# Eleven in place of ten one-hot tables for the first two blocks of a recommendation tower, with the third block's layers, the row numbers and the last loads moved

## The reference

```python
e = jnp.stack([tbl_0[ids[:, 0]], ..., tbl_25[ids[:, 25]]], axis=1)      # (2048, 26, 128)
all_emb = jnp.concatenate([bottom_output[:, None, :], e], axis=1)       # 27 features
gram = jnp.einsum('bfd,bgd->bfg', all_emb, all_emb)
z = gram[:, _TRIU_I, _TRIU_J]                                           # 351 products
h = jnp.concatenate([z, r_bottom_output], axis=1)                       # 479
h = jnp.maximum(h @ W_top1 + b_top1, 0.0)                               # 512
h = jnp.maximum(h @ W_top2 + b_top2, 0.0)                               # 256
y = h @ W_top3                                                          # 1
```

## Time and profile before

| | |
|---|---|
| profiled execution, its own time | 374.2 us |
| span, first to last instruction | 372.4 us |
| TensorE matmul busy | 339.9 us (91%) |
| TensorE weight load busy | 274.7 us (74%) |
| VectorE busy | 237.7 us (64%) |
| ScalarE busy | 231.8 us (62%) |
| GpSimd busy | 255.2 us (69%), gathers 252.1 |
| mean granted TensorE clock | 0.977 |
| chain that ended last | GpSimd 35%, TensorE 29%, issue 16%, VectorE 14% |

### The profile page before, as it was taken

How to read it: one execution, slowest core, us unless ns; L and a number is a source line. 1 busy time by engine, 2 the same in 40 slices (tenths; PEclk the granted TensorE clock), 3 DMA queues, 4 the chain that set the end, 5 groups by cost and what they waited for, 6 DMA issues and landing times.

```text
span 372.4 us, 8273 instructions
## 1 busy us (share of the span) xinstructions
PE 339.9 (91%) x3348; PEld 274.7 (74%) x3348; DVE 237.7 (64%) x276; ACT 231.8 (62%) x297; POOL 255.2 (69%) x258
## 2 busy tenths in 40 slices
PE   0899999998799999999799998999999983979997
PEld 0688777776578788888687886786888682867776
DVE  2999999999658769988599962423352223221542
ACT  3599988787887849689978744355533562131322
POOL 5778777777777777777777877777777777740020
PEclk9999999999789999999899999999999998899999
DMA  7867787664848898788765637742696354221110
GB/s 209 231 200 213 200 242 230 196 186 138 276 133 257 340 316 220 227 243 238 235 154 166 211 107 226 296 116 67 168 323 216 74 135 130 52 79 44 39 43 2
DMA packets 48391, 66.86 MB, mean 180 GB/s; under 512 B 15874, under 2 KB 34820, under 8 KB 47842
## 3 DMA queue, kind: packets, MB, share of 16 engines
q1 hardware_dynamic: 40126, 49.46, 44.3%
q0 software_dynamic: 8064, 16.35, 15.9%
q10 hardware_dynamic: 164, 0.52, 0.4%
HBM read 52.37 MB, written 13.93 MB: 178 GB/s over the span
## 4 chain that ended last, share of the span: by engine, by line
POOL 35%; PE 29%; issue 16%; DVE 14%; ACT 3%; DMA 2%; SPq 0%; ACTq 0%; DVEq 0%
POOL rows L559 35%; DVE onehot L827 11%; PE acc L587 8%; PE acc L588 7%; PE gram L618 4%; PE acc L623 3%; PE acc L625 2%; PE acc L624 2%; PE turned L600 2%; DVE table_lo L819 2%; DMA row_number<-in_row_numbers 2%; PE acc L662 1%; DVE pairs_lo L819 1%; ACT h L717 1%; DMA rows<-in_tbl,index 1%
## 5 line engine op out<-in xcount | busy, mean ns | idle before, releaser
L559 POOL DMA_INDIRECT rows<-in_tbl,index x248 | 252.1, 1017 | 78.0 <-issue 75.0
L827 DVE TENSOR_SCALAR onehot<-wanted,row_number 125x1029 fp32r<-125x1029 int32 x126 | 153.2, 1278 | 9.5 <-PE acc L588 9.4
L587 PE MATMUL acc<-onehot,table_hi 125*128 125x512 f32 x336 | 137.0, 408 | 12.4 <-DVE onehot L827 10.8
L588 PE MATMUL acc<-onehot,table_lo 125*128 125x512 f32 x288 | 115.8, 402 | 0.0
L587 PEld LDWEIGHTS acc<-onehot,table_hi 125*128 125x128 f32 x336 | 64.7, 193 | 28.5 <-issue 10.8
L618 PEld LDWEIGHTS gram<-features 128*54 128x54 f32 x2048 | 59.5, 134 | 15.3 <-issue 11.5
L618 PE MATMUL gram<-features 128*54 128x52 f32 x2048 | 65.5, 220 | 2.7 <-ACT features L696 1.7
L717 ACT ACTIVATE h<-wanted,row_number 125x1029 f32<-125x1029 int32 x42 | 48.8, 1163 | 26.2 <-PE acc L588 24.3
L588 PEld LDWEIGHTS acc<-onehot,table_lo 125*128 125x128 f32 x288 | 55.9, 194 | 12.5
L600 PE MATMUL turned<-identity,rows 128*128 128x128 f32 x248 | 40.7, 293 | 12.5 <-DMA rows<-in_tbl,index 6.8
L720 ACT ACTIVATE onehot<-h,row_number 125x1029 fp32r<-125x1029 f32 x42 | 48.6, 1157 | 1.4
(11 more groups left out here) (45 smaller groups left out, 279.5 us busy)
## 6 DMA issues: line engine op xcount, KB each, us to landing
wanted<-in_onehot_ids SPq DMA_DIRECT2D x21, 514.5 KB, 4.6
parked<-staged SPq DMA_DIRECT2D x32, 256.0 KB
table_raw<-in_tbl SPq DMA_DIRECT2D x17, 448.0 KB
looked<-parked SPq DMA_DIRECT2D x2, 2816.0 KB
square<-products SPq DMA_DIRECT2D x64, 84.5 KB
rows<-in_tbl,index POOLq DMA_INDIRECT x248
looked<-parked SPq DMA_DIRECT2D x1, 2560.0 KB
pairs<-in_tbl SPq DMA_DIRECT2D x3, 448.0 KB
```

Source lines behind the costliest of these rows:

```text
L559: pool.indirect_dma_start(out=rows[:, n % ROWS_RING, i, :], out_offset=None, in_=gathered[f], in_offset=bass.IndirectOffsetOnAxis(ap=index ...
L587: pe.matmul(to, table_hi[0:ROW_PARTS, v % HIGH_RING, c, :], of, start=(c == 0), stop=False)
L588: last = pe.matmul(to, raw_table(v, low=True)[0:ROW_PARTS, c, :], of, start=False, stop=(c == CHUNKS - 1))
L827: dve.tensor_scalar(onehot[0:ROW_PARTS, columns_of(v, c)], ids_of(v, slice(0, ROW_PARTS)), row_number[0:ROW_PARTS, c:c + 1], None, ALU.is_ ...
```

## The change

The number of looked-up tables becomes eleven for all blocks, so blocks 0 and 1 have 15 gathers per tile too (240 in all) and there are 22 visits, eleven of them ahead of the first gram chunk. `LAYERS_AT` for the last block becomes 8 and `ROUNDED_BEFORE` becomes a value per block, 6 for the last. `row_number` is loaded by GpSimd, as its first instruction, and no longer by SyncE. Part 3's pairs are loaded after the last chunk of tile 14, for three tiles, and part 4's after the last chunk of tile 15, for that tile only. Of the last tile's four stores two are issued by SyncE and two by ScalarE.

```diff
--- before.py
+++ after.py
@@ -19,7 +19,7 @@
 
 
 ONEHOT = [3, 4, 9, 13, 14, 17, 20, 21, 22, 23, 24]
-LOOKUPS = (10, 10, 11, 11)
+LOOKUPS = (11, 11, 11, 11)
 ALWAYS, MOST = min(LOOKUPS), max(LOOKUPS)
 ONEHOT_ROWS = 1000
 CHUNKS = 8
@@ -121,14 +121,14 @@
 
 
 
-LAYERS_AT = (None, 10, 10, 10)
+LAYERS_AT = (None, 10, 10, 8)
 
 
 
 LOOKUPS_AMONG = (16, 8, 8, 8)
 
 
-ROUNDED_BEFORE = 8
+ROUNDED_BEFORE = (None, 8, 8, 6)
 
 
 def products_and_others():
@@ -217,12 +217,14 @@
 
 
 
+
+LAST_LOT = (len(PARTS) - 1, BLOCK_TILES - 1, BLOCK_TILES)
 PAIRS_AFTER = {}
 for b in range(BLOCKS - 1):
     PAIRS_AFTER["gram", (b + 1) * BLOCK_TILES - 1, 1] = (b, 0, EARLY_TILES)
     PAIRS_AFTER["gram", (b + 1) * BLOCK_TILES - 1, TILE_CHUNKS - 1] = (b, EARLY_TILES, BLOCK_TILES)
-PAIRS_AFTER["gram", TILES - 1, 1] = (len(PARTS) - 2, 0, EARLY_TILES)
-PAIRS_AFTER["gram", TILES - 1, TILE_CHUNKS - 1] = (len(PARTS) - 1, EARLY_TILES, BLOCK_TILES)
+PAIRS_AFTER["gram", TILES - 2, TILE_CHUNKS - 1] = (len(PARTS) - 2, 0, BLOCK_TILES - 1)
+PAIRS_AFTER["gram", TILES - 1, TILE_CHUNKS - 1] = LAST_LOT
 
 
 
@@ -491,7 +493,7 @@
 
                 sp.wait_ge(act_products, chunks_taken(ACT_CHUNKS, (t + 1) * TILE_CHUNKS))
                 sp.wait_ge(dve_products, chunks_taken(DVE_CHUNKS, (t + 1) * TILE_CHUNKS))
-                for s in range(PACK):
+                for s in range(PACK if t < TILES - 1 else HELD):
                     store_place(sp, t, s)
 
             def load_pairs(part, first, end):
@@ -505,7 +507,6 @@
 
             load_index(0)
             load_wanted(0)
-            sp.dma_start(row_number[:], row_numbers).then_inc(row_number_landed, 16)
             load_raw(1)
             load_wanted(1)
             load_raw(2)
@@ -544,6 +545,7 @@
 
         @block.gpsimd
         def _(pool):
+            pool.dma_start(row_number[:], row_numbers).then_inc(row_number_landed, 16)
             pool.memset(identity[:], 0.0).then_inc(identity_zero, 1)
             pool.wait_ge(identity_zero, 1)
             pool.affine_select(out=identity[:], in_=identity[:], compare_op=ALU.not_equal, fill=1.0,
@@ -565,7 +567,7 @@
                 pool.wait_ge(square_landed[t % PRODUCTS_RING], (t // PRODUCTS_RING + 1) * PACK * 16)
             pool.wait_ge(accumulated, FILL["layer1", last_on_tiles_of(part), M1 - 1] + 1)
             for i in range(SP_LOADS, len(TRIPLES)):
-                load_triple(pool, *PARTS[part], i, last_pairs_landed)
+                load_triple(pool, PARTS[part][0], *LAST_LOT[1:], i, last_pairs_landed)
 
         @block.tensor
         def _(pe):
@@ -701,6 +703,13 @@
                 act.wait_ge(grammed, t * TILE_CHUNKS + j + 1)
                 at_least(act, square_landed[t % PRODUCTS_RING], (t // PRODUCTS_RING) * PACK * 16)
                 take_products(nc.scalar.copy, t, j).then_inc(act_products, 1)
+
+            def store_rest(t):
+
+                act.wait_ge(act_products, chunks_taken(ACT_CHUNKS, (t + 1) * TILE_CHUNKS))
+                act.wait_ge(dve_products, chunks_taken(DVE_CHUNKS, (t + 1) * TILE_CHUNKS))
+                for s in range(HELD, PACK):
+                    store_place(act, t, s)
 
             def table_high_part(v):
                 act.wait_ge(raw_landed[raw_place(v)], raw_count(v))
@@ -796,6 +805,8 @@
                 elif kind == "gram":
                     if y in ACT_CHUNKS:
                         products_out(x, y)
+                    if (x, y) == (TILES - 1, TILE_CHUNKS - 1):
+                        store_rest(x)
                     if (x, y) == (BLOCK_TILES, 0):
                         act.wait_ge(w1_landed, 16)
                         nc.scalar.copy(w1_hi[:], w1_raw[:]).then_inc(weights_high, 1)
@@ -889,7 +900,7 @@
                     fill_slot0(x)
                 elif kind == "gram":
                     b, q = divmod(x, BLOCK_TILES)
-                    if b and q * TILE_CHUNKS + y == ROUNDED_BEFORE:
+                    if b and q * TILE_CHUNKS + y == ROUNDED_BEFORE[b]:
                         split_pairs(b - 1)
                     if y in DVE_CHUNKS:
                         products_out(x, y)
```

## The result

| | before | after |
|---|---|---|
| median of the comparison | 374.44 us | 381.60 us |
| ratio, 95% interval | | 1.0195 [1.0121, 1.0269] |
| the same kernel run again, with others | 374.16 us | 379.98 us, 1.0154 [1.0121, 1.0188] |
| profiled execution, own time / span | 374.2 / 372.4 | 381.6 / 379.8 |
| mean granted TensorE clock | 0.977 | 0.972 |

The change makes the kernel slower by 1.5 to 2% (the two intervals span 1.2 to 2.7%). The forecast was 375.6 us with a range up to 379.5; the time lies above it.

A forecast was written before the change was run, and what follows sets the result against it. TensorE's own work was taken to set the pace up to about 307 us, then the gathers to 334. Span 372.4 + 8.3 - 0.7 - 0.6 - 1.9 - 9.9 + 1.1 + 1.0 + 3.1 + 1.0 = 373.8, plus 1.8: 375.6 us, range 369 to 379.5.

The forecast's parts named there:

- the pause ahead of t7.3: End of block 0's grams: transposes t7.3, moved ahead of chunk G4.0, wait for a ScalarE copy, +1.1 us.
- The extra visit: Before the first gram chunk: one more table visit, paced by VectorE, costs +8.3 us, ends 7.7 and 8.9.
- The waits that go: Last block: TensorE's pauses and the low clock behind them go, all but two copy waits, -9.9 us.
- the pairs wait: Third block's first layer piece: TensorE waits for tile 11's split pairs, +3.1 us, ends 2.6 and 3.6, or 0.
- +1.0 for the clock: Third block's layer piece: TensorE's clock is low behind the wait for split pairs, +1.0 us.
- 2.3 forecast: Behind tile 11's last chunk: 15 fewer transposes at 0.155 us each, -2.3 us.
- The row numbers: Kernel start: loaded by GpSimd they land sooner, so VectorE's first split comes earlier, -1.9 us, ends 0 and -1.9.
- case 4: Kernel start: row numbers come no sooner, GpSimd's descriptors waiting for VectorE or starting slowly; 377.5 us, chance 0.11.
- One copy fewer ahead of the first chunk: Between last lead visit and first gram chunk: six transpose groups, not seven, save one ScalarE copy, -0.6 us.
- case 3: Clock falls at all three new pauses (t7.3, t11.3, layer piece), 1.5 us each; 379.1 us, chance 0.13.
- The pause at tile 11: Tile 11: t11.3 waits 1.7 us for t11.1's copy while a shorter copy wait disappears, +1.0 us.

The follow-up runs named there:

- The kernel after again: The changed kernel, unchanged, measured a second time against the kernel before: 379.98 us, ratio 1.0154 [1.0121, 1.0188].
- The table of six: Changed kernel, third block's layers at chunk 10, 9, 8, against the kernel before: ten tables for blocks 0 and 1 1.0002, 0.9954, 0.9849; eleven 0.9991, 1.0033, 1.0154.

## Why the prediction was wrong

The step that failed is block 0. Between its first chunk and block 1's the sum has one term, +1.1 for the pause ahead of t7.3, and 5.1 us were measured. It has nothing there for the clock, which it let fall only behind the layer piece, and nothing for a load that lands late. The two small gains ahead of it, -1.9 and -0.6, did not come either. By the rows of the table the miss is 1.1 + 1.2 + 4.0 - 0.3 = 6.0 us.

1. **The extra visit, +8.3: right.** 8.3 in the lead; the splits stand (76.12 - 51.25)/3 = 8.3 apart as in the earlier trace rows.
2. **The waits that go, -9.9, and the pairs wait, +3.1 with +1.0 for the clock: right.** From tile 11's last chunk on the terms add up to -8.1, and -8.1 was measured. It holds for the parts as well: with eleven tables and the layers at chunk 10 this stretch takes 63.6 us, 12.0 less than before (9.9 + 2.3 forecast), and the early layers add 3.9 (4.1 forecast). The layer was reached 320.90 - 313.3 = 7.6 us behind tile 11's last chunk (7.7 forecast) and its piece was done 14.2 behind it (13.8 forecast). The last gather started at 324.0, not 320.1: the first came 0.8 later and the spacing was 1.33. It didn't matter.
3. **The row numbers, -1.9: failed.** The load's landing was taken from the loads of pairs at the end (2.3 to 2.7 us), when the nearest row was another load of the start, `wanted`, 5.8 us after its issue. It landed 6.1 after its issue. The first visit started 0.8 earlier, and that scatters as much from kernel to kernel. 1.1 us too much. It is the outcome of case 4 (no sooner), but nothing shows the mechanism of that case: SyncE's loads of the same table landed as late.
4. **One copy fewer ahead of the first chunk, -0.6: failed.** ScalarE still makes five copies of turns between its last one-hot build and the first placing copy, as before. With six transposes fewer TensorE only waits longer for the same copies: 3.31 ahead of the transposes where 2.67 stood, and 1.57 ahead of the chunk where 0.26 stood. 1.2 us in all.
5. **Block 0, +1.1 forecast and +5.1 measured: the largest part of the miss.** From start to start on TensorE, the 5.1 are these. From G3.3 to G4.0, where the pause at t7.3 stands, +2.1: the pauses at t7.2 and t7.3 are 2.01 + 1.20 against 1.91, and t7.3's transposes, now ahead of G4.0, took 0.88. The low clock at the first two chunks, +0.9, and in the visit behind them, +0.5 (8.14 against 7.64). At and in the fourth visit +1.8: a wait of 0.49 for the split of a table and one of 0.73 for ScalarE's copy of an accumulator. The rest is -0.2. The last two causes stay open. For the low clock see "The kernel after again". The table landed late, but that doesn't follow from the change: its cast comes 2.1 us behind the start of the two chunks ahead (146.81 - 144.66) and 0.3 before, yet 2.7 with ten tables and the layers at chunk 8 and 0.5 with ten tables and the layers at chunk 10, two kernels with the same steps up to there.
6. **The clock.** "After a pause of 1.91 the granted clock was 0.73" was held to be one place; I counted a fall only behind the layer piece. It fell behind t7.3 too, to 0.54 and for longer than before, but not behind tile 11's pauses of 0.41 and 1.20, where it was 1.00. Against the kernel before, the fall at t7.3 costs 1.3 us more (about 2.5 against 1.2; 1.0 of it shows in G4.0 and the visit behind it, 11.0 us against 10.0). So case 3 had the mechanism right at two of its three places and a fair price, 1.5, for one. That its 379.1 is the nearest to the measured time is mostly luck, since most of the miss lies elsewhere. The Trainium skill, TensorE: Matmul & The Clock Gate, section "HAM oscillation — how this bites in real kernels", tells of a kernel in which each wait for data between two groups of matmuls brings the low level back. Its waits are longer than the three new pauses here, of which two were followed by a fall and one was not.
7. **The pause at tile 11, +1.0: right in size.** The pauses are 0.41 and 1.20. From G7.3 to G8.0 it takes 3.2 us more, of which 1.7 are the eleven moved transposes; a copy wait of 0.67 behind it is gone; 0.8 are left. That the whole stretch to tile 11's last chunk grew by 2.4, near the 2.7 forecast, is partly luck: 1.0 of it is the low clock behind block 1's start, and block 1's first layer piece took 1.4 less than before, since it no longer waits 1.47 us for its pairs. Keeping all the pulled turns back gained 3.4 us in the medians, against 2.1 for the two terms without a clock behind them.

The sum subtracted the waits for rows for the tables and charged the layers a wait. For both parts together that was right. What it never asked is what either would do without the other. The table of six shows that either alone would have been the better change.

## What to carry to other kernels

When a change holds two remedies for one wait, cost each alone and both together: here the early layers were worth 1.5% with the waits for rows, and cost 1.6% without them. A pause that is made longer or split in two next to an existing one is priced by the clock of the stretch behind both, taken from the row of the existing pause as a lower end. A load's landing is taken from the nearest load of the same time of the program. And a difference between two profiles is put down to an edit only where the steps differ: 2.3 to 3.0 us here lay where they were the same.

## What was not expected of the hardware

- Behind pauses of 2.01 and 1.20 us with four transposes between them the granted clock was 0.50 for 5.5 us. With a gram chunk and its 32 matmuls in between, and 2.04 and 0.29 of pause, it was 0.73 over the same length; behind the one pause of 1.91 in the kernel before, 0.69. Behind 0.41 and 1.20, with four transposes between them, it was 1.00.
- A load of a small table issued at 1.3 us by GpSimd landed 6.1 to 7.1 us later; the same load issued at 1.7 by SyncE landed 5.7 to 6.5 later. GpSimd's loads at the end took 2.4. Whether the start of the program makes the difference or the other loads is not separated here: the core's DMA engines were busy for 0.79 of the time from 2 to 4 us and all of it from there to 7.4, and for 0.25 of it from 355 to 362 us.
- A table's load can land 2 us later in one kernel than in another with the same steps up to there, and TensorE then waits for it in the middle of a stretch that it otherwise paces.
